# Small attention on one core: the value projection one place later, normalising ahead of it, and the last batch's outputs taken late into two other banks

## The chip, the cores and the metric

The kernel runs on one core of a Trainium2 chip. The metric is the device time of one execution in microseconds (us), as the median of several runs. Below, TensorE is called PE, VectorE DVE, ScalarE ACT, GpSimd POOL, and SyncE, which issues the DMAs, SP.

## The reference, cut to what matters

The reference is a stack of four pairs of cross attention and feed forward over x of 8 x 128 x 512. The change touches one member alone, the small attention of the second pair (L1): 8 batches, 4 patches of 128 columns, 8 heads of width 8.

```python
q = einsum('ed,bdw->bew', Wq, qp) + bq[:, None]      # 64 x 128 of each patch
k = einsum('ed,bdw->bew', Wk, qp) + bk[:, None]
val = einsum('ed,bdw->bew', Wv, vp) + bv[:, None]
scores = einsum('bhdi,bhdj->bhij', qh, kh) / sqrt(dh)
scores = where(mp[:, :, None, :] > 0, scores, -1e9)
o = einsum('bhij,bhdj->bhdi', softmax(scores), vh)
out = einsum('de,bew->bdw', Wo, gelu(o)) + bo[:, None]
x = x + out * masks
```

## The kernel before, in words

The whole program keeps x (8 batches of 128 x 512) in SBUF and runs eight stages one after the other. Each engine has its own instruction stream in program order, written out by hand; semaphores join them. Nothing is reordered by a planner, so a wait that is not met holds everything behind it on its engine.

**The small attention.** Work is cut into 64 units, `UNITS` = 8 for each of 8 batches; unit u is patch n and half s of the heads (4 heads at a time) of batch u // 8. Below, "place i" is u % 8. On PE each place does, in this order: the scores of unit u (L1972); an extra for the next batch (`extras`, L2011); the turning of the probabilities of unit u - 2 (L1980); on even u the values and row sums of the two units u - 4 and u - 3 (L1997, L2000); and at place 6 `spread_inverse` of the batch before (L2008). The extras of the next batch are: places 0 and 1 the keys' projection (L1952), places 2 and 3 the queries' (L1957), place 5 the values' (`project_v`, L1964). `project_v` waits for `q_low`, since it writes the bank proj[0] that DVE's `low_of_queries` reads. The next batch's `project_k` of half 0 writes the same bank and so waits for `v_made`, which DVE's `take_values` gives.

**DVE** does at each place `maxima` (L2181), at odd places `take_turned` (L2187, the copy of the turned probabilities of unit u - 2), then its extras: places 0 and 1 `take_keys` (L2160), place 3 `invert` (L2191), places 4 and 5 `low_of_queries` (L2165), place 6 `take_values` (L2174, L2175) and `norm` (L2153, the input of the batch after next), place 7 `normalise` (L2196). `normalise` of a batch waits for `spread_inverse` and for ACT's `take_outputs`.

**ACT** does `exps` (L2086) at each place, at even places `take_turned` (L2093), and as extras `high_of_keys` (L2073) at 1 and 2, `high_of_queries` (L2078) at 3 and 4, `take_outputs` (L2118) at 5; in batch 3 also three roundings for the next stage at 5, 6 and 7.

**POOL** makes the low parts of the keys (L1915), the live mask (L1897) and the eight blocked key tiles of a batch (L1928), which the scores read. Before the blocks of a batch it waits for the dead-key rows that SP loads (L1861). For the last batch SP issues those rows only after `v_full` has counted all 8 value projections (L1882).

**The end of the stage.** After the last unit PE runs `spread_inverse(7)`, and then `pe_tail` (L596): eight output products (L2049) into outp[0] and outp[1] in turn, each after its product's mask weighing by POOL (L1939), which follows ACT's gelu (L2142), and after DVE's addition two batches before (L500). `out_product(1)` waits for all `onorm`, as outp[1] is also the bank that `normalise(7)` reads. `UNREAD_EXIT` puts four matmuls whose result nobody reads (`unread_passes`, L590: 128x512 of the context into proj[0]) ahead of products 0, 1 and 7. In `dve_tail` (L656) the first half's reciprocal root (`dve_ln_rstd`, scratch in proj[1]) stands between the additions 4 and 5; it waits for ACT's deviations of batches 0 to 3 (L506), which stand behind the gelus in ACT's order.

Of the kernel before, what the change touches and what calls it, by code (L numbers as in the profile page):

```python
# [16 lines left out]
B = 8  # L17
S = 128
D = 512
# [237 lines left out]
def build(nc, ins, out):  # L257

    with ExitStack() as ctx:
# [332 lines left out]
        UNREAD_OUT = {B - 1: 4}  # L592
        UNREAD_EXIT = {0: 4, 1: 4, B - 1: 4}
        UNREAD_TURN = {2: 5, 3: 2}
# [61 lines left out]
        def dve_tail(dve, n, add_of):  # L656
# [7 lines left out]
            if n == 3:  # L664
                dve_ln_rstd(dve, n, 0, proj[1][:, 0:BH], proj[1][:, BH:B])
            else:
                dve_ln_rstd(dve, n, 0)
            for b in range(BH + 1, B):
                add_of(b)
            if n == 3:  # L670
                dve_ln_rstd(dve, n, 1, proj[1][:, B:B + BH], proj[1][:, B + BH:2 * B])
            else:
                dve_ln_rstd(dve, n, 1)
# [1144 lines left out]
        o1 = [flat[0:E1, b * D:(b + 1) * D] for b in range(B)]  # L1818
        turn1, made1 = [turn, outp[0]], [heado, outp[1]]
        tail_mask = [tbuf[0:E1, b, :] for b in range(2)] + [ring[0:E1, 4 + b, :] for b in range(2)] + \  # L1820
# [120 lines left out]
        def l1_pe(pe):  # L1941
# [69 lines left out]
            def extras(b, i):  # L2011
                if b + 1 >= B:
                    return
                if i < 2:
                    project_k(b + 1, i)
                elif i < 4:
                    project_q(b + 1, i - 2)
                elif i == 5:
                    project_v(b + 1)

            for s in range(2):
                project_k(0, s)
# [5 lines left out]
            for u in range(UNITS * B):  # L2028
                scores(u)
                extras(u // UNITS, u % UNITS)  # L2030
                if u >= 2:
                    turn_probabilities(u - 2)
                if u >= 4 and u % 2 == 0:
                    values(u - 4)
                if u >= UNITS and u % UNITS == 6:
                    spread_inverse(u // UNITS - 1)
            u = UNITS * B
# [3 lines left out]
            values(u - 2)  # L2041
            spread_inverse(B - 1)

            def out_product(b):
                if b == 1:
                    pe.wait_ge(m["onorm"], B)
                pe.wait_ge(m["weighed"], b + 1)
                wait(pe, m["added"], b - 1)
                pe.matmul(outp[b % 2][:, :], wo1, flat[0:E1 + 1, b * D:(b + 1) * D], start=True, stop=True)\  # L2049
                  .then_inc(m["out_full"], 1)  # L2050
# [3 lines left out]
        def l1_act(act):  # L2054
# [83 lines left out]
            take_turned(UNITS * B - 2)  # L2138
            take_outputs(B - 1)
            for b in range(B):  # L2140
                act.wait_ge(m["onorm"], b + 1)
                act.activation(o1[b], o1[b], ACT.Gelu, bias=vecs[0:E1, V_BV1:V_BV1 + 1]).then_inc(m["gelu"], 1)  # L2142
# [4 lines left out]
        def l1_dve(dve, add_of):  # L2147
# [50 lines left out]
            def extras(b, i):  # L2198
                if b + 1 < B:
                    if i < 2:  # L2200
                        take_keys(b + 1, i)
                    elif i in (4, 5):
                        low_of_queries(b + 1, i - 4)
                    elif i == 6:
                        take_values(b + 1)
                if b + 2 < B and i == 6:
                    norm(b + 2)
                if b and i == 3:
                    invert(b - 1)
                if b and i == 7:  # L2210
                    normalise(b - 1)

# [20 lines left out]
            invert(B - 1)  # L2233
            normalise(B - 1)

            def add(b):
                dve.wait_ge(m["out_full"], b + 1)
                dve_add_sum(dve, b, outp[b % 2][:, :]).then_inc(m["added"], 1)
                dve.wait_ge(m["added"], b + 1)
# [488 lines left out]
```

## Time and profile before

| what | value |
|---|---|
| runs shown | 2985.66, 2993.47, 2994.1 us; median 2993.47 |
| profiled execution, own time | 2991.93 us |
| span of its trace | 2990.3 us |
| PE busy | 2904.1 us (97%) |
| DVE, ACT, POOL busy | 56%, 38%, 33% |
| mean granted clock of PE | 0.995 of full |
| the small attention in the span | about 1102.4 to 1274.5 us |

The profile is one execution; times in it are counted from the start of its span, and the 1.6 us between its span and its own time lie around the program. The small attention is about 172 us, or 6% of the span. Outside it the program is bound by large products on PE; the change does not touch them.

### The profile page before, as it was taken

The numbers are of one execution on the slowest core, as the hardware profiler recorded it, in microseconds if no ns is written. First come the engines' busy times: TensorE is split into PE (matmuls) and PEld (weight loads), VectorE is DVE, ScalarE is ACT, GpSimd is POOL, SyncE is SP. The second block draws the span as 40 slices with busy tenths as digits, with TensorE's granted clock in tenths as the row PEclk, the third lists the DMA queues.
The fourth block names the chain that finished last, engine by engine and source line by source line (L and its number), as shares of the span: only waits on it lengthen the run. The fifth ranks groups of instructions, "written<-read, shape, count | busy, mean of one in ns | idle before, by whom it ended". The sixth has DMA issues, their size and how long they took to land.

```text
span 2990.3 us, 48856 instructions
## 1 busy us (share of the span) xinstructions
PE 2904.1 (97%) x16710; PEld 2450.0 (82%) x16710; DVE 1682.1 (56%) x3414; ACT 1126.0 (38%) x3642; POOL 988.8 (33%) x822
## 2 busy tenths in 40 slices
PE   7999999999999998899999999999999999999999
PEld 6888888888888866578778888888778888888787
DVE  6544545445452247678766666666764444445644
ACT  4322222222242237732354444444443333333432
POOL 3433333433313227543333222332232333332221
PEclk9999999999999999999999999999999999999999
DMA  3111111111111111011111001110011111110111
GB/s 122 45 49 42 44 34 41 48 41 45 40 36 57 34 45 30 26 39 39 40 40 33 29 28 35 35 35 18 26 57 36 36 35 35 35 35 21 46 49 46
DMA packets 68761, 120.32 MB, mean 40 GB/s; under 512 B 8697, under 2 KB 14329, under 8 KB 68257
## 3 DMA queue, kind: packets, MB, share of 16 engines
q1 hardware_dynamic: 68642, 118.76, 13.0%
q8 instruction: 71, 1.16, 0.2%
q14 instruction: 48, 0.39, 0.0%
HBM read 116.57 MB, written 2.10 MB: 40 GB/s over the span
## 4 chain that ended last, share of the span: by engine, by line
PE 90%; DVE 5%; ACT 2%; issue 2%; POOL 1%; DMA 0%; DVEq 0%; SPq 0%; POOLq 0%; ACTq 0%
PE proj L394 42%; PE outp L394 25%; PE heado L1012 6%; PE score L971 6%; PE turn L998 3%; PE score L394 2%; PE proj L410 1%; PE proj L938 1%; PE score L1558 0%; PE score L1972 0%; PE turn L921 0%; PE proj L1957 0%; PE proj L1952 0%; PE outp L1980 0%; PE outp L1997 0%
## 5 line engine op out<-in xcount | busy, mean ns | idle before, releaser
L394 PE MATMUL outp<-w_out,acts 128*128 128x512 f32 x3288 | 841.3, 400 | 11.0 <-DVE acts L1702 4.4
L394 PE MATMUL proj<-xnT,w_in 128*128 128x512 f32 x3192 | 760.0, 393 | 2.0 <-ACT big L1076 2.0
L394 PEld LDWEIGHTS outp<-w_out,acts 128*128 128x128 f32 x3288 | 594.1, 188 | 140.3 <-DVE x L1697 8.9
L394 PEld LDWEIGHTS proj<-xnT,w_in 128*128 128x128 f32 x3192 | 594.5, 189 | 126.3 <-issue 2.2
L394 PE MATMUL proj<-ctxT,w_kv 128*128 128x512 f32 x1536 | 366.0, 394 | 19.3 <-POOL w_kv L728 18.2
L726 POOL TENSOR_TENSOR w_out<-ring,consts 128x512 fp32r<-128x512 f32 x96 | 102.4, 1067 | 820.8 <-PE outp L394 820.8
L394 PEld LDWEIGHTS proj<-ctxT,w_kv 128*128 128x128 f32 x1536 | 286.7, 189 | 78.4 <-issue 18.1
L1303 DVE TENSOR_TENSOR x<-x,outp 128x512 f32<-128x512 f32 x360 | 244.8, 685 | 181.7 <-PE outp L394 178.6
L1079 DVE COPY big<-proj 128x512 f32<-128x512 f32 x136 | 93.7, 689 | 343.0 <-PE proj L394 338.8
L1076 ACT ACTIVATE big<-proj 128x512 f32<-128x512 f32 x136 | 81.4, 598 | 475.8 <-PE proj L394 469.3
L726 POOL TENSOR_TENSOR w_kv<-ring,consts 128x512 fp32r<-128x512 f32 x93 | 96.6, 1039 | 465.1 <-DMA ring<-in_L_wk 444.6
L1174 ACT ACTIVATE acts<-heado 128x512 fp32r<-128x512 f32 x192 | 114.7, 597 | 309.3 <-PE heado L1012 309.2
L1309 DVE TENSOR_TENSOR acts<-heado,acts 128x512 fp32r<-128x512 f32 x192 | 132.7, 691 | 148.5 <-ACT acts L1174 148.4
L1012 PEld LDWEIGHTS heado<-ptbuf,big 128*128 128x128 f32 x1536 | 200.7, 191 | 17.9 <-ACT ptbuf L1162 1.0
L1162 ACT ACTIVATE ptbuf<-turn 128x512 f32<-128x512 f32 x192 | 114.3, 595 | 266.9 <-PE turn L998 266.8
L1012 PE MATMUL heado<-ptbuf,big 128*128 128x128 f32 x1536 | 202.3, 274 | 1.0 <-DVE acts L1309 1.0
L971 PEld LDWEIGHTS score<-big 128*128 128x128 f32 x1536 | 184.4, 193 | 9.4 <-issue 4.7
L971 PE MATMUL score<-big 128*128 128x128 f32 x1536 | 188.8, 276 | 3.0 <-issue 1.7
L394 PE MATMUL proj<-w_kv,ctxT 128*128 128x256 f32 x1536 | 183.1, 280 | 0.9 <-DVE big L1079 0.9
L394 PEld LDWEIGHTS proj<-w_kv,ctxT 128*128 128x128 f32 x1536 | 182.1, 188 | 2.3 <-DVE big L1079 1.1
L1697 DVE TENSOR_TENSOR x<-x,outp 128x512 f32<-128x512 f32 x152 | 104.2, 686 | 92.1 <-PE outp L394 92.0
L726 POOL TENSOR_TENSOR w_in<-ring,consts 128x512 fp32r<-128x512 f32 x96 | 106.1, 1106 | 118.5 <-PE proj L394 65.8
(338 smaller groups left out, 4093.3 us busy)
## 6 DMA issues: line engine op xcount, KB each, us to landing
ring<-in_L_wq SPq DMA_DIRECT2D x96, 256.0 KB, 2.6
ring<-in_L_wo SPq DMA_DIRECT2D x96, 256.0 KB, 2.6
ring<-in_F_in SPq DMA_DIRECT2D x52, 256.0 KB, 2.7
ring<-in_L_wk SPq DMA_DIRECT2D x48, 256.0 KB, 2.6
ring<-in_L_wv SPq DMA_DIRECT2D x48, 256.0 KB, 3.3
ring<-in_F_out SPq DMA_DIRECT2D x41, 256.0 KB, 2.6
x<-in_x SPq DMA_DIRECT2D x2, 1024.0 KB, 8.0
big<-in_ctxT SPq DMA_DIRECT2D x4, 512.0 KB, 7.6
```

Of the source, the lines that this page charges most:

```text
L394: mm = pe.matmul(bank_ap, w_ap(a, c), rhs(b, c), start=first and c == 0 and n == 0, stop=last and c == chunks - 1 and n == len(PASSES) - 1)
L726: pool.tensor_tensor(dst[:, slot, 0, :], ring[:, r, :], zeros512, ALU.add).then_inc(m["high_w"], 1)
L971: mm = pe.matmul(score[half][:, b * P:(b + 1) * P], qT[:, t], kT[:, t], start=True, stop=True)
L998: mm = pe.transpose(turn[:, b * P:(b + 1) * P], probs[j % 2][:, half, b * P:(b + 1) * P], ident)
L1012: mm = pe.matmul(heado[:, b * P:(b + 1) * P], v_pair[:, n, j % 2, :] if A.own_kv else v[:, n * S:(n + 1) * S], ptbuf[:, half, b * P:(b + 1 ...
L1076: return engine.activation(dst, src, ACT.Copy)
L1079: return engine.tensor_copy(dst, src)
L1162: act.activation(ptbuf[:, half, :], turn[:, :], ACT.Copy).then_inc(m["tfree"], 1)
L1174: act.activation(acts[:, j, 0, half * HALF:(half + 1) * HALF], heado[:, :], ACT.Copy)\
L1303: dve.tensor_tensor(x[:, b, :], x[:, b, :], outp[b % 2][:, :], ALU.add).then_inc(m["added"], 1)
L1309: dve.tensor_tensor(acts[:, j, 1, cols], heado[:, :], acts[:, j, 0, cols].bitcast(F32), ALU.subtract)\
L1697: dve.tensor_tensor(x[:, b, :], x[:, b, :], outp[b % 2][:, :], ALU.add).then_inc(m["added"], 1)
```

## The change

On PE `project_v` moves from place 5 to place 6 and `spread_inverse` from place 6 (behind the values) to place 5 (ahead of the turning). On DVE `take_values` moves from place 6 to place 7, behind `take_turned`, and `normalise` from place 7 to place 6, ahead of `norm`. Eight unread matmuls stand ahead of the first key projection, and those ahead of output products 0 and 1 go. The last batch's `spread_inverse` and `normalise` stand between output products (additions) 1 and 2, its `take_outputs` ahead of its own gelu and behind the seven others. The output products use outp[0] and proj[1] in place of outp[0] and outp[1]; the scratch of the reciprocal root changes places with them.

```diff
--- before.py
+++ after.py
@@ -590,7 +590,7 @@
                 pe.matmul(proj[0][:, :], ctxT[:, 0, 0, 0:P], ctxT[:, 0, 0, 0:HALF], start=True, stop=True)
 
         UNREAD_OUT = {B - 1: 4}
-        UNREAD_EXIT = {0: 4, 1: 4, B - 1: 4}
+        UNREAD_EXIT = {B - 1: 4}
         UNREAD_TURN = {2: 5, 3: 2}
 
         def pe_tail(pe, n, out_of):
@@ -662,13 +662,13 @@
                     add_of(b)
                 return
             if n == 3:
-                dve_ln_rstd(dve, n, 0, proj[1][:, 0:BH], proj[1][:, BH:B])
+                dve_ln_rstd(dve, n, 0, outp[1][:, 0:BH], outp[1][:, BH:B])
             else:
                 dve_ln_rstd(dve, n, 0)
             for b in range(BH + 1, B):
                 add_of(b)
             if n == 3:
-                dve_ln_rstd(dve, n, 1, proj[1][:, B:B + BH], proj[1][:, B + BH:2 * B])
+                dve_ln_rstd(dve, n, 1, outp[1][:, B:B + BH], outp[1][:, B + BH:2 * B])
             else:
                 dve_ln_rstd(dve, n, 1)
             dve_ln_norm(dve, n, 4)
@@ -1816,7 +1816,7 @@
         mask1, dead1 = ring[E1:E1 + B, 4, :], ring[E1:E1 + B, 5, :]
         krows = spare[STACK:ROWS, :].rearrange("p (k s n) -> p k s n", k=2, s=2)
         o1 = [flat[0:E1, b * D:(b + 1) * D] for b in range(B)]
-        turn1, made1 = [turn, outp[0]], [heado, outp[1]]
+        turn1, made1, out1 = [turn, outp[0]], [heado, outp[1]], [outp[0], proj[1]]
         tail_mask = [tbuf[0:E1, b, :] for b in range(2)] + [ring[0:E1, 4 + b, :] for b in range(2)] + \
                     [tail1[0:E1, b * D:(b + 1) * D] for b in range(2)] + \
                     [factors1[0:E1, 14 * P + b * D:14 * P + (b + 1) * D] for b in range(2)]
@@ -2015,9 +2015,10 @@
                     project_k(b + 1, i)
                 elif i < 4:
                     project_q(b + 1, i - 2)
-                elif i == 5:
+                elif i == 6:
                     project_v(b + 1)
 
+            unread_passes(pe, 8)
             for s in range(2):
                 project_k(0, s)
             for s in range(2):
@@ -2028,25 +2029,24 @@
             for u in range(UNITS * B):
                 scores(u)
                 extras(u // UNITS, u % UNITS)
+                if u >= UNITS and u % UNITS == 5:
+                    spread_inverse(u // UNITS - 1)
                 if u >= 2:
                     turn_probabilities(u - 2)
                 if u >= 4 and u % 2 == 0:
                     values(u - 4)
-                if u >= UNITS and u % UNITS == 6:
-                    spread_inverse(u // UNITS - 1)
             u = UNITS * B
             turn_probabilities(u - 2)
             values(u - 4)
             turn_probabilities(u - 1)
             values(u - 2)
-            spread_inverse(B - 1)
 
             def out_product(b):
-                if b == 1:
-                    pe.wait_ge(m["onorm"], B)
+                if b == 2:
+                    spread_inverse(B - 1)
                 pe.wait_ge(m["weighed"], b + 1)
                 wait(pe, m["added"], b - 1)
-                pe.matmul(outp[b % 2][:, :], wo1, flat[0:E1 + 1, b * D:(b + 1) * D], start=True, stop=True)\
+                pe.matmul(out1[b % 2][:, :], wo1, flat[0:E1 + 1, b * D:(b + 1) * D], start=True, stop=True)\
                   .then_inc(m["out_full"], 1)
 
             pe_tail(pe, 3, out_product)
@@ -2136,8 +2136,9 @@
                     take_turned(u - 2)
                 extras(u // UNITS, u % UNITS)
             take_turned(UNITS * B - 2)
-            take_outputs(B - 1)
             for b in range(B):
+                if b == B - 1:
+                    take_outputs(b)
                 act.wait_ge(m["onorm"], b + 1)
                 act.activation(o1[b], o1[b], ACT.Gelu, bias=vecs[0:E1, V_BV1:V_BV1 + 1]).then_inc(m["gelu"], 1)
             ffn_act_first(act, F1)
@@ -2201,14 +2202,14 @@
                         take_keys(b + 1, i)
                     elif i in (4, 5):
                         low_of_queries(b + 1, i - 4)
-                    elif i == 6:
+                    elif i == 7:
                         take_values(b + 1)
+                if b and i == 6:
+                    normalise(b - 1)
                 if b + 2 < B and i == 6:
                     norm(b + 2)
                 if b and i == 3:
                     invert(b - 1)
-                if b and i == 7:
-                    normalise(b - 1)
 
             for b in range(BH + 2):
                 add_of(b)
@@ -2231,11 +2232,12 @@
                     dve_ln_rstd(dve, 2, 1, outp[1][:, 0:BH], outp[1][:, BH:B])
             take_turned(UNITS * B - 1)
             invert(B - 1)
-            normalise(B - 1)
 
             def add(b):
+                if b == 2:
+                    normalise(B - 1)
                 dve.wait_ge(m["out_full"], b + 1)
-                dve_add_sum(dve, b, outp[b % 2][:, :]).then_inc(m["added"], 1)
+                dve_add_sum(dve, b, out1[b % 2][:, :]).then_inc(m["added"], 1)
                 dve.wait_ge(m["added"], b + 1)
 
             dve_tail(dve, 3, add)
```

## Rows read from the trace of the kernel before

**Rows 1.** The page: busy time of each engine, and the chain that ended last.
```profile
PE 2904.1 (97%) x16710; PEld 2450.0 (82%) x16710; DVE 1682.1 (56%) x3414; ACT 1126.0 (38%) x3642; POOL 988.8 (33%) x822
PE 90%; DVE 5%; ACT 2%; issue 2%; POOL 1%; DMA 0%; DVEq 0%; SPq 0%; POOLq 0%; ACTq 0%
```

**Rows 2.** By stretch: length; busy PE, weight loads, DVE, ACT, POOL; clock; DMA, GB/s.
```profile
1130.72:1218.67 87.95, 80.13 (x962) 55.87 (x961) 67.69 (x104) 71.42 (x209) 63.18 (x56) 1.00 0.09 26
...
1268.45:1275.27 6.82, 6.82 (x14) 3.73 (x14) 4.27 (x19) 3.74 (x8) 6.42 (x6) 0.50 0.07 13
```

**Rows 3.** Order of time on PE, one batch: start, length, operation, idle time before it.
```profile
1148.00 1.02 PE L1952 MATMUL proj<-sq,wk 128*96 128x512 f32 x2
...
1158.34 0.49 PE L1972 MATMUL score<-stacks 98*128 98x512 f32 x1
...
1159.83 1.08 PE L1964 MATMUL proj<-biasbuf,ring 128*128 128x64 f32 x8 [0.99 <-DVE stacks L2165]
...
1165.26 1.02 PE L1952 MATMUL proj<-sq,wk 128*96 128x512 f32 x2
```

**Rows 4.** Order of time on DVE, the end of the same batch.
```profile
1156.49 0.69 DVE L2187 COPY ptbuf<-outp 128x512 f32<-128x512 f32 x1 [0.61 <-PE outp L1980]
1157.22 0.96 DVE L2191 RECIPROCAL inverse<-outp 64x128 f32<-64x128 f32 x1
1158.21 0.69 DVE L2181 TENSOR_REDUCE negmax<-score 128x4 f32<-128x512 f32 x1
...
1162.11 0.75 DVE L2165 SCALAR_TENSOR_TENSOR stacks<-proj,biasbuf,stacks 32x512 fp32r<-32x512 f32 x1
1162.89 0.69 DVE L2181 TENSOR_REDUCE negmax<-score 128x4 f32<-128x512 f32 x1
1163.50 0.35 DVE L2174 COPY spread<-proj 128x192 f32<-128x192 f32 x1
...
1164.01 0.64 DVE L2153 TENSOR_SCALAR sq<-x,rstd,recentre 128x512 f32<-128x512 f32 x1
...
1166.11 0.69 DVE L2196 TENSOR_TENSOR big<-big,outp 64x512 f32<-64x512 f32 x1
```

**Rows 5.** Order of time on ACT, the same end of batch.
```profile
1158.93 1.14 ACT L2086 ACTIVATE pbuf<-score,negmax 128x128 f32<-128x128 f32 x4 [0.68 <-DVE negmax L2181]
...
1160.42 0.69 ACT L2078 ACTIVATE stacks<-proj,biasbuf 96x512 fp32r<-96x512 f32 x1
...
1162.46 0.59 ACT L2118 ACTIVATE big<-outp 64x512 f32<-64x512 f32 x1
```

**Rows 6.** Order of time on SP, POOL and PE where the last batch begins.
```profile
1231.61 2.51 SPq L1861 DMA_DIRECT2D spare<-ring  x4
...
1236.34 6.03 POOL L1928 TENSOR_TENSOR stacks<-spare,consts 98x512 fp32r<-98x512 f32 x6 [7.98 <-issue]
...
1237.44 0.56 PE L1972 MATMUL score<-stacks 98*128 98x512 f32 x1 [1.57 <-POOL stacks L1928]
```

**Rows 7.** Busy time by stretch, right behind that wait (columns as in rows 2).
```profile
1237.70:1241.10 3.40, 3.40 (x38) 2.47 (x38) 0.69 (x1) 1.42 (x5) 3.40 (x4) 0.51 0.72 236
```

**Rows 8.** Order of time on PE, the start of the stage and the middle of batch 0.
```profile
1104.44 3.53 PE L1952 MATMUL proj<-sq,wk 128*96 128x512 f32 x4 [2.06 <-DMA pattern<-in_L_pattern]
...
1124.56 1.44 PE L1964 MATMUL proj<-biasbuf,ring 128*128 128x64 f32 x8 [2.84 <-DVE stacks L2165]
```

**Rows 9.** Order of time on ACT, PE and DVE, the end of the stage.
```profile
1254.93 0.60 ACT L2093 ACTIVATE ptbuf<-turn 128x512 f32<-128x512 f32 x1 [0.75 <-PE outp L2000]
...
1258.07 1.28 ACT L2142 ACT_TABLE_LOAD   x1
...
1259.49 1.21 PE L590 MATMUL proj<-ctxT 128*128 128x512 f32 x4
...
1272.55 1.91 PE L2049 MATMUL outp<-big,biasbuf 65*128 65x512 f32 x2
...
1274.56 0.69 DVE L500 SCALAR_TENSOR_TENSOR x<-outp,x 128x512 f32<-128x512 f32 x1 [2.06 <-PE outp L2049]
```

## The prediction

> **What bounds the kernel now.** I read the page first, then the stretches of the stage, then the order of time of one batch on each engine. The page says that PE is busy for 97% of the span and carries 90% of the chain that ended last [rows 1]. So the change can only gain where PE waits inside the small attention, and only lose by making PE wait or run slower there. The five stretches from the key projection of one batch to that of the next, for batches 2 to 7, take 87.95 us at full granted clock with PE busy for 80.13 of them [rows 2]. One undisturbed batch is 1148.00 to 1165.26, or 17.26 us. Its largest hole on PE is ahead of the value projection: the scores of place 5 start at 1158.34 and, by the spacing of such scores, let PE go on 0.34 us later, but the value projection starts at 1159.83, released by DVE's `low_of_queries` [rows 3]. That is 1.15 us, and the trace calls 0.99 of it idle. The reader is to see two more things in these rows. The copy of the values on DVE starts at 1163.50 and takes about 0.56 us (0.51 to the start of `norm`) [rows 4], while the key projection that needs it starts at 1165.26, so it has 1.2 us in hand. And DVE's and ACT's operations of places 3 to 6 follow each other almost without a gap [rows 4, 5].
>
> **The change, part by part.** Times with a + are counted from a batch's first key projection.
>
> *The hole ahead of the value projection.* With `spread_inverse` at place 5, PE has about 1.0 us of work where it waited (its eight matmuls keep the same cost; they only move). The inverse is ready: DVE's reciprocal ran 1157.22 to 1158.18, ahead of the scores of place 5. The turning follows, then the scores of place 6, which wait some 0.2 us for the exponentials of place 4 (ACT 1158.93 plus 1.14, rows 5), and then the value projection finds `low_of_queries` done. PE would reach the next key projection at 17.26 - 1.15 + 0.25 = +16.4. If nothing else were late, five batches would gain 0.9 each, 4.5 us.
>
> *What is late next.* The key projection needs `v_made`. I follow DVE from the last point that PE alone sets, the turning at place 3. It releases `take_turned` at 1156.49 - 1148.00 = +8.49, `invert` starts 0.73 later, `maxima` of place 4 follows after 0.99, ACT's exponentials after 0.72, the queries' high part after 1.49 (with a copy between) and it takes 0.69 [rows 4, 5]. So `low_of_queries` of half 1 starts at +13.15. In the trace it started at 1162.11, +14.11, behind a late `take_turned`, so this is 0.96 earlier. Then come `maxima` of place 6 (at +13.93, 0.61 to the next) and, new here, `normalise`. It needs ACT's `take_outputs`, which follows place 5's exponentials (from about +13.1, 1.02 to the next) and ends at +14.7. So: `normalise` +14.74 (0.72), `norm` +15.46 (0.64), `maxima` of place 7 +16.10 (0.61), `take_turned` +16.71 (0.73), and only then `take_values` +17.44, done at +18.0. I allow 0.1 for the crossing to PE: the key projection starts at +18.1. PE has waited 1.7 us for it, and the batch is 0.87 us longer than before. Behind that wait on PE stand a turning, values and the scores of place 1. From there to place 3 DVE and ACT are earlier relative to PE than before, and PE sets the pace again, so the loop settles at 18.1. Five such stretches give 90.6 against 87.95: **+2.7 us**. Batch 3, where ACT has three more roundings, is already slower and hides a part of its own share. Bounds: -4.5 (the copy never late) and +4.4 (0.87 everywhere).
>
> *The clock.* In the trace one wait of this size stands in the stage: PE idles 1.57 us ahead of the scores of unit 56 [rows 6], and right behind it 3.40 us run at 0.51 of the full clock, the 1.2 GHz level [rows 7]. Work that takes half of that at full clock is done in it, so such a drop costs 1.7 us where PE sets the pace. The waits of 0.99 did not do it: all five stretches show 1.00 [rows 2]. The new wait of 1.7 is nearest to the one of 1.57. But its batch has different work around it each time, and one case is one case: I take three drops of five, **+5.1 us**, bounds 0 and 8.5.
>
> *The start.* PE idles 2.06 us ahead of the first key projection, and the four matmuls behind it take 3.53 us where two of them take 1.02 at full clock [rows 3, 8]. Four matmuls of 128x512 that nobody reads took 1.21 us at the end of the stage [rows 9]; eight fit about into the idle 2.06 and should hold the clock. Two key projections, query projections and their DVE steps then end earlier, and POOL's blocks start about 1.2 us earlier. It does not last. Batch 0 contains a reciprocal root on DVE that holds PE for 2.84 us [rows 8] in either order, and in the new order the values are copied behind `take_turned` there too; by the same steps the next batch's key projection comes out where it was. **0**, bounds -1.3 and +0.6.
>
> *The DMAs of the last batch.* The dead-key rows of batch 7 are queued on SP behind the last value projection: issue at 1231.61, POOL's blocks from 1236.34, the scores of unit 56 at 1237.44 [rows 6]. The value projection ends at +13.66 instead of +12.9, so rows, blocks and scores come 0.7 us later relative to their batch: **+0.7**. PE's wait there grows from 1.57 to about 3.5 us, and the slow stretch behind it may be longer: bounds 0 and +2.4. SP's later loads stand behind these; they are for the next stage, which needs them only behind the gelus.
>
> *The end.* `spread_inverse(6)` no longer stands between values and the scores of unit 63, which brings the last units about 0.95 us forward. ACT can load its gelu table right behind `take_turned` (1254.93 plus 0.60) instead of at 1258.07 [rows 9], so the gelus, and POOL behind them, start 3.5 us earlier. The end of the stage is the addition of batch 7 at 1274.56. It waits for its product, this for addition 5, this for the reciprocal root, this for ACT's deviations of batch 3, and these for the gelu of batch 7, which now waits for `normalise(7)` between additions 1 and 2. With the granted clock at full this walk ends at 1271.5, a gain of 3.1. But without the unread matmuls PE has only short products with gaps between them; the trace had 6.82 us at half clock there even with them [rows 2], where one product took about 1.7 us (1.91 for its two records, rows 9), which is slower than POOL weighs the batches. If the clock is low from the second product on, PE sets the pace with eight products, the spreading and the last four unread ones, and the gain is 0.5. I take a value nearer to that: **-1.2**, bounds -3.1 and +1.7 (one more slow stretch). The two other banks cost nothing and free the first product from `normalise(7)`; the scratch only changes places.
>
> Sum: 2.7 + 5.1 + 0 + 0.7 - 1.2 = **+7.3 us** on the profiled execution's own 2991.93, or 2999.2. The median of the runs shown is 2993.47, 1.5 us above that execution, and the runs spread over 8 us; about 0.3% (9 us) is what a measurement of this kernel can tell from no change. I forecast **2999 us**, no change that can be told, on the slow side of it.
>
> **The rivals.**
> *A. No drops of the clock.* The new wait stays short of what lowers it. For it: the waits of 0.99 never did. Against it: 1.57 did. Sum 2.7 + 0.7 - 1.2 = +2.2, or 2994.
>
> *B. A drop in every batch: slower.* The place is the first key projection of batches 3 to 7; the price is 1.7 us each, 8.5 in all, and it decides once more than three fall. For it: the wait is longer than the one that did it. Sum 2.7 + 8.5 + 0.7 - 1.2 = +10.7, or 3002.6, slower by 0.36%.
> The Trainium skill, "TensorE: Matmul & The Clock Gate", section "A second HAM failure mode: psum-queue depth-cycling", says that PE can swing between its two clock levels when it idles briefly and often between groups of matmuls. By that rule every batch would pay, as in B. The trace so far goes against it at 0.99 us of idle per batch.
>
> *C. The copy is not late: faster.* DVE's chain has slack that I do not see, PE keeps the 4.5 us, the start keeps 1.3 and the end 3.1: -8.9, or 2983.0, faster by 0.30%. Against it: the steps above add up rows that follow each other without gaps, and 1.7 us would have to be wrong.
>
> *D. The reordering does nothing*, as its waits are all covered elsewhere: 2992. PE's share of the chain speaks against it.
>
> **How the numbers follow.** Forecast with some drops 0.36, A 0.26, B 0.22, C 0.12, D 0.04. C comes out at the bound, so with the runs' own spread, and a little for what no case names, about 0.11 is faster by over 0.3%. B, and the forecast where it falls high, give 0.30 slower; 0.59 is within. The range takes in A, B and most of C, with the bounds of the end: 2984 to 3007.
>
> **What would show it.** Right: the value projection without a DVE wait ahead of it; ahead of L1952 in each batch a wait of 1.5 to 1.9 us released by DVE's `take_values` (L2175 before); batches of 18.1 us; half clock behind some of these waits; at the start full clock; the wait for POOL ahead of unit 56 near 3.5 us; the gelu table load ahead of the last `take_outputs`. Wrong: batches below 17 us, which would mean that DVE reaches the copy earlier than the walk says; full clock throughout, which leaves A; or a stage that ends over 3 us earlier, counted from its last values, which would mean that the end is worth more than I gave it.

## The result, and the profile after

The changed kernel takes 3028.5 us (median of 4 runs, 3021.49 to 3032.6) against 2993.48 for the kernel before: 1.0121 of its time, 95% interval 1.0094 to 1.0147. It is slower by some 35 us, and the forecast of 2999 with its range up to 3007 missed it. The profiled execution of the changed kernel took 3032.6 us, its span 3031.0.

The page of the changed kernel, which answers to [rows 1], with the total above them and the first PE group of its costliest groups (busy time, mean ns, idle time ahead of it and what ended it):

```profile
span 3031.0 us, 48854 instructions
PE 2924.6 (96%) x16710; PEld 2463.7 (81%) x16710; DVE 1679.3 (55%) x3414; ACT 1125.3 (37%) x3642; POOL 988.9 (33%) x822
q14 instruction: 73, 0.60, 0.1%
PE 87%; DVE 6%; issue 3%; ACT 2%; POOL 1%; DMA 0%; DVEq 0%; SPq 0%; ACTq 0%; POOLq 0%
L394 PE MATMUL outp<-w_out,acts 128*128 128x512 f32 x3288 | 848.9, 402 | 32.3 <-DVE x L1303 24.2
```

The same lines of the kernel before, for the total, the queue that carries instructions (packets, MB, share) and that group:

```profile
span 2990.3 us, 48856 instructions
q14 instruction: 48, 0.39, 0.0%
L394 PE MATMUL outp<-w_out,acts 128*128 128x512 f32 x3288 | 841.3, 400 | 11.0 <-DVE acts L1702 4.4
```

The numbers of matmuls and of DVE, ACT and POOL operations are the same as in [rows 1]. What differs is odd for a change of order in the small attention: PE now idles 32.3 us ahead of output products of the *large* members (L394), 24.2 of it for DVE's addition L1303; "issue", time in which an engine waits for nothing that the profile shows, goes from 2% to 3% of the chain; and the queue that brings instructions moved 73 packets, where it moved 48.

The waits (engine, what it did next, whom it waited for: us in all, times, longest) say where. First the stretch 1640 to 2182 us of the changed kernel, which is the attention with 8 groups of 4 heads behind F1:

```profile
ACT pbuf L1136 <- DVE negmax L1254: 38.2, 12, 7.1
DVE pbuf L1248 <- issue: 31.8, 5, 6.8
PEld outp L394 <- DVE x L1303: 25.5, 13, 5.0
PE outp L394 <- DVE x L1303: 22.6, 7, 4.8
```

and the same of the kernel before (1600 to 2140):

```profile
ACT pbuf L1136 <- DVE negmax L1254: 9.1, 13, 0.9
DVE pbuf L1248 <- DVE rq L442: 3.9, 12, 0.6
PE outp L394 <- DVE x L1303: 1.0, 2, 0.9
```

DVE stands still 5 times, 31.8 us together, ahead of L1248, and ACT and then PE wait behind it. The order of time on DVE shows one of them, and the starts of all five:

```profile
1687.06 0.17 DVE L442 SCALAR_TENSOR_TENSOR rq<-heado,rq 128x8 f32<-128x8 f32 x1
1693.28 1.13 DVE L1248 SCALAR_TENSOR_TENSOR pbuf<-score,rq,maskadd 128x128 f32<-128x128 f32 x4 [6.05 <-issue]
1694.44 0.69 DVE L1254 TENSOR_REDUCE negmax<-pbuf 128x4 f32<-128x512 f32 x1
...
1781.18 1.13 DVE L1248 SCALAR_TENSOR_TENSOR pbuf<-score,rq,maskadd 128x128 f32<-128x128 f32 x4 [6.83 <-issue]
...
1867.75 1.13 DVE L1248 SCALAR_TENSOR_TENSOR pbuf<-score,rq,maskadd 128x128 f32<-128x128 f32 x4 [6.72 <-issue]
...
1954.72 1.12 DVE L1248 SCALAR_TENSOR_TENSOR pbuf<-score,rq,maskadd 128x128 f32<-128x128 f32 x4 [6.11 <-issue]
...
2040.89 1.13 DVE L1248 SCALAR_TENSOR_TENSOR pbuf<-score,rq,maskadd 128x128 f32<-128x128 f32 x4 [6.13 <-issue]
```

They are 86 to 88 us apart, one for each round of the loop that runs groups 1 to 6 of this attention. Six rounds have five jumps back, and this L1248 is the first operation of the loop's body. PE shows it as some 5 us more of idle time in each 100 (columns as in [rows 2]). The kernel before has

```profile
1700.00:1800.00 100.00, 99.04 (x571) 85.71 (x571) 63.06 (x178) 46.38 (x214) 31.72 (x27) 1.00 0.11 31
```

and the changed one

```profile
1700.00:1800.00 100.00, 94.33 (x531) 81.77 (x530) 60.61 (x175) 41.19 (x187) 23.70 (x20) 0.96 0.10 27
1800.00:1900.00 100.00, 94.47 (x520) 81.35 (x519) 57.48 (x160) 42.20 (x188) 23.68 (x20) 0.97 0.08 27
```

The granted clock (third number from the end) is lower as well. Over the five stretches from 1600 to 2100, PE idles 26.8 us in the changed kernel and 5.2 in the one before, and the clock is 0.96 to 0.98 where it was 1.00. So some 22 us of the loss are PE's idle time; the rest is work behind these waits at the lower clock, by my estimate from these rows 14 us (500 us at 0.03 less).

From the first L1248 of this attention to its last, the kernel before takes 601.8 us (1515.9 to 2117.7), the changed one 635.7 (1524.5 to 2160.2). That is 33.9 of the 40.7 us between the two spans, in a stage whose text the change does not touch. A further 8.6 lie ahead of it, 2.8 of them ahead of the first key projection's start in the small attention (1104.44 against 1107.24), and e6, which has no part of the change there, starts as late (1107.36).

**The theory.** The page's total is 2 instructions lower (48854 for 48856). Counted in the compiled program, one of them is PE's, a dropped wait, and the other is DVE's. In the changed kernel the two waits of `normalise(B - 1)` share one wait instruction, and the addition behind it has lost one of its two waits to the normalising ahead of it and needs no instruction for the other. So everything on DVE behind the small attention lies one instruction earlier, the loop of 264 instructions too (its register addition and its jump are counted). It is the only loop outside PE's program that is longer than 256; DVE's other four have 66 to 142. Theory M: DVE keeps a part of its program at hand and loads the rest in blocks. At this start the loop no longer fits in what is kept, and each jump back must load again. The Trainium skill, "Runtime: NRT & Kernel Launch", section "Instruction fetch mechanics", says that most engines (TensorE has more) hold 512 instructions, in two blocks of 256, and that a taken jump to what is not held waits for a load. By that rule 264 instructions touch three blocks from 7 of 256 starts. The rival, N: what the small attention does differently reaches the later stage as a shift in time.

### The profile page after: what moved, and what is told of

Same layout as the page of the kernel before. It is cut to its first block, busy times and chain, and to the rows that moved or that the text cites. A ratio compares the mean times of both kernels' runs of the same rounds, so it can differ in the third digit from the quotient of the medians.

```text
span 3031.0 us, 48854 instructions
## 1 busy us (share of the span) xinstructions
PE 2924.6 (96%) x16710; PEld 2463.7 (81%) x16710; DVE 1679.3 (55%) x3414; ACT 1125.3 (37%) x3642; POOL 988.9 (33%) x822
## 4 chain that ended last, share of the span: by engine, by line
PE 87%; DVE 6%; issue 3%; ACT 2%; POOL 1%; DMA 0%; DVEq 0%; SPq 0%; ACTq 0%; POOLq 0%
PE proj L394 40%; PE outp L394 24%; PE heado L1012 6%; PE score L971 5%; PE turn L998 3%; PE score L394 2%; PE proj L410 1%; DVE pbuf L1248 0%; PE score L1558 0%; PE score L1972 0%; ACT acts L1174 0%; PE proj L1952 0%; DVE acts L1309 0%; PE heado L1997 0%; PE proj L1957 0%
## 5 line engine op out<-in xcount | busy, mean ns | idle before, releaser
L394 PE MATMUL outp<-w_out,acts 128*128 128x512 f32 x3288 | 848.9, 402 | 32.3 <-DVE x L1303 24.2
L394 PE MATMUL proj<-xnT,w_in 128*128 128x512 f32 x3192 | 761.2, 394 | 2.0 <-ACT big L1076 2.0
L394 PEld LDWEIGHTS outp<-w_out,acts 128*128 128x128 f32 x3288 | 598.6, 190 | 164.4 <-DVE x L1303 28.4
L394 PEld LDWEIGHTS proj<-xnT,w_in 128*128 128x128 f32 x3192 | 595.5, 189 | 126.6 <-issue 2.3
L394 PE MATMUL proj<-ctxT,w_kv 128*128 128x512 f32 x1536 | 366.8, 395 | 19.6 <-POOL w_kv L728 18.6
L394 PEld LDWEIGHTS proj<-ctxT,w_kv 128*128 128x128 f32 x1536 | 287.1, 189 | 79.1 <-issue 18.6
L1303 DVE TENSOR_TENSOR x<-x,outp 128x512 f32<-128x512 f32 x360 | 244.2, 685 | 183.8 <-PE outp L394 180.7
L394 PE MATMUL proj<-w_kv,ctxT 128*128 128x256 f32 x1536 | 183.1, 280 | 0.9 <-DVE big L1079 0.9
L394 PEld LDWEIGHTS proj<-w_kv,ctxT 128*128 128x128 f32 x1536 | 182.0, 188 | 2.3 <-DVE big L1079 1.1
```

The source lines that it names most:

```text
L394: mm = pe.matmul(bank_ap, w_ap(a, c), rhs(b, c), start=first and c == 0 and n == 0, stop=last and c == chunks - 1 and n == len(PASSES) - 1)
L1303: dve.tensor_tensor(x[:, b, :], x[:, b, :], outp[b % 2][:, :], ALU.add).then_inc(m["added"], 1)
```

## The experiments

The last column is the time from the first L1248 of that attention to the last, from the two ends in each profile. "DVE ahead" is the number of DVE's instructions ahead of its loop, counted in the compiled programs, against the kernel before. In the session of e13 to e15 the kernel before took 2992.82 us, one run.

| run | DVE ahead | loop | time to before (95%) | issue ahead of L1248, us, times | q14 packets | L1248 first to last |
|---|---|---|---|---|---|---|
| before | 0 | 264 | 1 | none | 48 | 601.8 |
| after | -1 | 264 | 1.0121 (1.0094, 1.0147) | 31.8, 5 | 73 | 635.7 |
| e1 after, one wait more | 0 | 264 | 1.0034 (1.0023, 1.0044) | none | 48 | 600.5 |
| e2 before, one wait less | -1 | 264 | 1.0103 (1.0086, 1.0120) | 30.7, 5 | 73 | 631.8 |
| e3 before | -11 | 264 | 0.9997 (0.9987, 1.0006) | none | 47 | 600.6 |
| e4 after, one more behind the loop | -1 | 264 | 1.0124 (1.0106, 1.0141) | 31.2, 5 | 73 | 632.9 |
| e9 before, unread start | -9 | 264 | 1.0002 (0.9993, 1.0012) | none | 47 | 600.5 |
| e10 before | -8 | 264 | one run, 2990.42 | none | 47 | 600.5 |
| e13 before | -7 | 264 | one run, 3011.97 | 27.4, 10 | 72 | 627.3 |
| e14 before | +248 | 264 | one run, 3012.3 | none | 49 | 600.4 |
| e15 before | +249 | 264 | one run, 3044.34 | 27.5, 10 | 74 | 630.6 |
| e11 after, shorter loop | -1 | 248 | 1.0018 (1.0009, 1.0027) | none | 47 | 601.5 |
| e16 before, shorter loop | 0 | 248 | 1.0000 (0.9991, 1.0009) | none | 47 | 599.9 |

### One instruction

e1 is the changed kernel with one wait that is long met:

```diff
             take_turned(UNITS * B - 1)
+            dve.wait_ge(m["sfull"], UNITS * B)
             invert(B - 1)
```

> The changed kernel with one more DVE instruction, a wait that is long met, ahead of the last reciprocal of the small attention. Theory M (instruction fetch): the change leaves DVE's program one wait instruction shorter, which moves the 264-instruction loop of the big attention that follows across a boundary of the instruction store, and each of the 5 jumps back then waits some 6.4 us (31.8 us in 5 in the changed kernel's waits). M expects that wait gone and about 2997 us (3028.5 less 32). Rival N (what the small attention does differently reaches the later stage as a shift in time): one wait that is met at once changes nothing, 3028 us with the 5 waits still there.

e2 is the kernel before with one wait less, in `norm`:

```diff
-                dve.wait_ge(ln_rms, centred(2, b // BH))
+                if b != 2:
+                    dve.wait_ge(ln_rms, centred(2, b // BH))
```

> The kernel before with one DVE wait instruction fewer (the input of batch 2 no longer waits for the reciprocal root that batch 0 has already waited for); nothing else of the change. M expects 5 waits of 6.4 us ahead of L1248 and about 2993.5 + 32 = 3025 us. N expects no such wait and 2993 us.

e3 drops this wait for five batches, and in the last additions six waits of DVE on its own additions (`if b in (BH, B - 1)` ahead of the trailing wait on `added`).

> The kernel before with 11 DVE wait instructions fewer (waits that an earlier wait of DVE has met already). M with a store refilled in blocks of 256: a loop of 264 touches three blocks only for the 8 or 9 starts just ahead of a boundary, so minus one to minus nine would be slow and minus eleven is back at about 2993 us with no wait. If instead every shorter program were slow, it would be some 3025 us. N expects 2993 us, as for minus one.

e4 has two waits on L1's `added` and `out_full` ahead of the last additions of the attention behind the loop, which make one more instruction there.

> Control: the changed kernel with one more DVE wait instruction behind the loop of the big attention in place of ahead of it, so the program is as long as in the kernel before but the loop lies where it does in the changed one. M expects 3028 us with the 5 waits; only if the program's whole length counted would it be 2997 us. N expects 3028 us too.

e1 takes 2997.55 us, 31 less than the changed kernel, for one instruction more; e4, timed beside it, takes 3026.29, so 28.7 more than e1. The group of L1248 in its profile (idle time ahead of it, times):

```profile
  DVE rq L442: 6.5, 25
```

e2, which has nothing of the change, pays for one instruction less:

```profile
  issue: 30.7, 5
  DVE rq L442: 3.7, 20
```

M holds in all four and N in neither of the two where they differ. PE's program is one instruction shorter in e1 too, which is clean, and not in e2, which is slow, so its length is not the cause. e3 says that a shorter program is not slow by itself, and e4 that the whole length does not count, only what stands ahead of the loop.

### Which starts are slow

e10 and e13 leave out eight and seven of e3's waits (five of `norm`, and three and two of the additions); e14 and e15 add them:

```diff
             take_turned(UNITS * B - 1)
+            for k in range(248):
+                dve.wait_ge(m["sfull"], UNITS * B)
+                dve.wait_ge(m["exps"], UNITS * B)
             invert(B - 1)
```

> The kernel before with 8 met DVE wait instructions fewer. It marks the edge of the bad starts beside minus nine and minus eleven: if the jump at the loop's end counts (265 instructions), three blocks are still touched and the 5 waits are there (about 3020 us); if 264 count, it is clean (about 2990 us). If both minus eight and minus nine are clean, M holds but the edge lies nearer to minus one.

> The kernel before with 7 met DVE wait instructions fewer. Minus one is slow and minus eight is clean. If the store is refilled in blocks of 256 and the loop's 264 instructions are what must fit into two blocks, starts minus one to minus seven are slow and minus eight is the first clean one: 5 waits of 6 to 7 us ahead of L1248, about 3020 us. If the slow starts are only the one or two next to the boundary (a first instruction too late in its block), minus seven is clean at 2990 us.

> The kernel before with 248 more DVE wait instructions, all met, ahead of the last reciprocal of the small attention: that costs DVE some time there, the same within a wait as in plus 249. Blocks of 256: 248 more is minus eight of the next block, so no wait of 6.4 us ahead of L1248. Blocks of another size (128, 512): nothing special at either of the two.

> As plus 248 with one more. Blocks of 256: 249 more is minus seven of the next block, so 5 waits of 6 to 7 us ahead of L1248 and some 31 us more than plus 248. Blocks of 512: as plus 248, no such wait. Blocks of 128 would have shown at plus 121 and be silent here unless the loop needed two of a different count: then both or neither.

Minus seven is slow and minus eight is clean (e3's and e9's expectations had put the edge one or two further); plus 249 is slow and plus 248 is clean. The additional waits of e14 cost time at their own place (the last normalising starts at 1284.0 in place of 1259.6), in e15 as well; between the two lie 32.0 us for one instruction. So slow starts were seen at -1, -7 and +249, clean ones at 0, -8, -9, -11 and +248, and the pattern comes again after 256. That is what two blocks of 256 and a body of 264 give if the loop of the kernel before starts on the first instruction of a block (its place in the store is inferred from the pattern, not read): up to seven earlier leave 257 or more for the blocks behind, and eight earlier fit again. The Trainium skill's rule, in the section named above, agrees with these starts to the instruction.

At -7 and +249 the wait is split. e13's group of L1248 has

```profile
  issue: 27.4, 10
```

and in the order of time the first of its rounds:

```profile
1676.76 1.13 DVE L1248 SCALAR_TENSOR_TENSOR pbuf<-score,rq,maskadd 128x128 f32<-128x128 f32 x4 [4.36 <-issue]
1679.72 1.13 DVE L1248 SCALAR_TENSOR_TENSOR pbuf<-score,rq,maskadd 128x128 f32<-128x128 f32 x4 [1.11 <-issue]
```

Seven instructions at the end of a block give DVE something to do before it needs the next block; with one it waits some 6.4 us in one piece. That the split comes from two loads one after the other is my reading of it.

### The loop's length

e11 is the changed kernel, its loop at the same bad start, but 16 instructions shorter:

```diff
-                m.wait(dve, "added", B * p + (b - B + 1))
+                if A.layer != 2 or isinstance(p, int):
+                    m.wait(dve, "added", B * p + (b - B + 1))
```

> The changed kernel, its loop of the big attention at the same start, but the loop 248 instructions long in place of 264: inside it DVE's additions no longer wait for its own additions of 8 steps before (PE's products already wait for them). M: two blocks hold 248 instructions at that start, so the 5 waits go, and it is 2997 us or a little less (16 instructions in each of 6 rounds fewer). If the start by itself is what costs (its first instruction the last of a block), the waits stay and it is 3028 us.

> The kernel before with the shorter loop of e11 (248 instructions in place of 264, DVE's additions in the big attention not waiting for its own of 8 steps before). At before's start the loop was clean already, so the theory of the store expects no gain from that; what is left is 16 instructions fewer in each of 6 rounds on an engine that PE seldom waits for: 0 to -0.001 of before. If the shorter loop is what took the changed kernel from 1.0034 (with the wait) to 1.0018 (with the short loop), this one is 0.998 to 0.999; if that difference was scatter, it is 1.000.

The waits are gone at the bad start: the length of the body, with its start, decides. With blocks of 256, a body of up to 257 would fit two blocks from every start, an estimate from the edges above, so this repair does not hang on what stands ahead. e16 shows that the 16 instructions are worth nothing by themselves (1.0000).

### The parts of the change

These were made at clean starts, so they show what the change does in its own stage.

> The kernel before with only the value projection a place later (and the spread of the inverse, the values' copy and the normalising moved as in the change); the start, the end and the banks are those of before, and DVE's program keeps its length. My prediction's steps: +2.7 us for the wait of the next key projection on the values' copy, +5.1 for clock drops, so about 2990 + 6 to 8. The marks of the changed kernel (last key projection 120.9 after the first, where before has 117.4) say +3.5 to +4. If the move is a gain by itself (the start or the end of the stage being the loss), it would be 2987 or less.

> The kernel before with only the end changed: last batch's outputs taken late, output products in the two other banks, no unread matmuls ahead of products 0 and 1; one met DVE wait keeps the program's length. My prediction's step: -1.2 us (bounds -3.1 and +1.7). The marks of the changed kernel say -2.4 up to the first output product and +4 to +4.4 from there to the last one, so +1.5 to +2.

> As the end alone, but the 4 unread matmuls ahead of output products 0 and 1 stay. If the loss at the end is the half clock of the products (1.06 us each where before has 0.68), this one keeps the clock up and has the gain of the late outputs alone: 1 to 2.5 us faster than before. If the loss is the new order (normalising the last batch behind the first additions), the unread matmuls change nothing and it is as the end alone, +1.5 to +2.

> The changed kernel with one met DVE wait (program length of before) and DVE's copy of the values ahead of its copy of the turned probabilities at place 7. My prediction's rival C: the key projection then does not wait (some 1.0 us less in each of the 7 batches, up to 5 us in all, and fewer clock drops), so 4 to 8 us below the changed kernel with the wait alone (1.0034 of before), i.e. 0.9993 to 1.001 of before. If what costs is the turned copy, which PE's values wait for, it moves the hole there and the time stays at 1.003.

> The kernel before with the 8 unread matmuls ahead of the first key projection as its only part of the change, and 9 met DVE wait instructions fewer. My prediction's step for the start: 0 (bounds -1.3 and +0.6). What the parts leave open: the changed kernel with the wait is 1.0034 of before, the value move alone 1.0019, the end alone 0.9998, so the start would be +0.0015 or +4.5 us if parts add. Theory M with a store in blocks of 256 and a loop of 264 or 265: nine fewer is the first start at which two blocks hold the loop again, so no wait of 6.4 us ahead of L1248.

> Value projection at place 6 with DVE's copy of the values ahead of its turned copy, the late outputs in the two other banks with the unread matmuls ahead of products 0 and 1 kept, no unread matmuls at the start, and the shorter loop of e11. By the parts: copy ahead 0 to -1, end -1 to 0, start 0, the loop's 16 fewer instructions 0 to -3, so 0.998 to 1.000 of before. If the parts don't add (the phase of the stages behind shifts), 1.000 to 1.002.

> The kernel before with the value move of e5 and DVE's copy of the values ahead of its turned copy, and nothing else. e5 is 1.0019 with stretches of 17.78 us; in e8 they were 17.18 with the copy ahead (before: 17.26). So 7 batches at -0.1 us: 0.999 to 1.000 of before. If the wait of the key projection was not what made e5 slower, it stays at 1.002.

e5, e6 and e9 are the hunks of the change one at a time; e7 is e6 with `UNREAD_EXIT` as before. The copy ahead, in e8, e12 and e17, is this, with `take_values` gone from place 7 of `extras`:

```diff
                 maxima(u)
+                if u % UNITS == 7 and u // UNITS + 1 < B:
+                    take_values(u // UNITS + 1)
                 if u >= 2 and u % 2:
                     take_turned(u - 2)
```

| run | time to before (95%) | five stretches, us | last scores to first L1558 of the next stage |
|---|---|---|---|
| before | 1 | 87.95 | 35.5 |
| e1 whole change, clean start | 1.0034 (1.0023, 1.0044) | 91.65 | 37.5 |
| e5 value move alone | 1.0019 (1.0010, 1.0027) | 90.01 | 34.3 |
| e6 end alone | 0.9998 (0.9989, 1.0006) | 87.92 | 37.5 |
| e7 end, unread kept | 1.0001 (0.9992, 1.0010) | 87.97 | 34.6 |
| e8 whole change, copy ahead | 1.0004 (0.9996, 1.0013) | 87.58 | 37.6 |
| e9 start alone | 1.0002 (0.9993, 1.0012) | 87.92 | 34.2 |
| e12 copy ahead, end with unread, short loop | 1.0001 (0.9992, 1.0010) | 87.60 | 34.7 |
| e17 value move, copy ahead | 1.0014 (1.0005, 1.0023) | 89.23 | 37.3 |

The value move is the part that costs, 5.7 us (0.0019 of 2989). That is a little less than the 6 to 8 of my steps and more than the 3.5 to 4 that the key projections in the changed kernel's trace had said. The end and the start cannot be told from zero (-3.3 to +1.8 us, and -2.1 to +3.6); for the end I had expected +1.5 to +2. With the new order of the end, the unread matmuls of the exit hold the clock, as the stretch of the output products shows (the clock is the third number from the end), in e6, which leaves those ahead of products 0 and 1 out:

```profile
1260.50:1278.00 17.50, 17.47 (x30) 8.05 (x31) 7.65 (x28) 11.03 (x24) 13.31 (x11) 0.51 0.09 30
```

and in e7, which has them:

```profile
1257.70:1272.00 14.30, 11.27 (x37) 5.49 (x38) 8.02 (x29) 10.05 (x23) 13.26 (x11) 1.00 0.07 18
```

By the profiles they are worth 2.9 us at the end of the stage (37.5 against 34.6), but the timed runs do not tell e7 from e6, so my expectation of 1 to 2.5 us below before was wrong there. The column's 35.5 for the kernel before is one execution: in nine profiles whose end is that of the kernel before it lies between 34.2 (e9, e13) and 37.3 (e17), by which of its products run at half clock (so with the order of before the same matmuls do not hold it each time). So a comparison with one profile of before says little, while the 37.5 to 37.6 (e1, e6, e8) and the 34.6 to 34.7 (e7, e12) repeat. With the copy ahead, e8's stretches come out at 87.58, just below before's, and the time is before's. e17 has the same copy and is 1.0014; its profile has one stretch where the first key projection and the next are 4.41 us apart (1201.64 to 1206.05) where the others need 2.79, that is one clock drop of 1.6 us. My expectation was 0.999 to 1.000. Its interval and e8's overlap, and why it should lie above e8 by more than that drop is open. So is why the whole change at a clean start is 1.0034 with the long loop and 1.0018 with the short one (these intervals overlap too), when the parts sum to 1.0019 and e16 gives the short loop nothing. No version beats the kernel before by what can be measured.

## Why the prediction was wrong, point by point

**The step that failed** is the sentence ahead of the sum: "the change can only gain where PE waits inside the small attention, and only lose by making PE wait or run slower there". The sum had no term for an engine's instruction stream outside the stage. One DVE instruction less put the 264-instruction loop of a later attention on a bad start, where five jumps back wait 31.8 us, for 26 to 31 us of the time (1.0121 against e1's 1.0034 is 26 us; the medians of the two, 3028.5 and 2997.55, differ by 31; e4 less e1 is 28.7, and e2's 1.0103 is 30.8). The walk should have counted what the change adds and drops in each engine's program, waits too, and looked behind the stage for loops near the limit. None of the rivals had it either: B, the slower one, is a clock rule.

**Inside the stage** the sum of +7.3 us stands against +10.2 (e1, interval 6.9 to 13.2) and +5.4 (e11, 2.7 to 8.1). Its steps, in the changed kernel's trace:

*Late copy of the values.* The order came out as walked. DVE at the end of a batch whose first key projection is at 1134.49, against [rows 4]:

```profile
1149.26 0.69 DVE L2197 TENSOR_TENSOR big<-big,heado 64x512 f32<-64x512 f32 x1
1149.87 0.54 DVE L2154 TENSOR_SCALAR sq<-x,rstd,recentre 128x512 f32<-128x512 f32 x1
1150.43 0.69 DVE L2182 TENSOR_REDUCE negmax<-score 128x4 f32<-128x512 f32 x1
1151.04 0.68 DVE L2188 COPY ptbuf<-outp 128x512 f32<-128x512 f32 x1
1151.64 0.35 DVE L2175 COPY spread<-proj 128x192 f32<-128x192 f32 x1
```

`normalise` is at +14.77 (walked +14.74) and `take_turned` at +16.55 (+16.71); the copy is at +17.15 where I had +17.44, because `norm`, `maxima` and the copy follow the operations ahead of them at 0.61, 0.56 and 0.60 us where I took 0.72, 0.64 and 0.73. PE, against [rows 3]:

```profile
1168.31 0.47 PE L1972 MATMUL score<-stacks 98*128 98x512 f32 x1
1170.04 1.07 PE L1952 MATMUL proj<-sq,wk 128*96 128x512 f32 x2 [1.25 <-DVE spread L2176]
```

The stretch is 17.78 us (1152.26 to 1170.04), not 18.1, and the wait 1.25, not 1.7. The value projection no longer waits (in all batches L1964 waited 9.8 us for L2165 in the kernel before, and 1.1 in the changed one, in one batch), so the hole was closed and a larger one opened behind it, as predicted.

*The copy never late (rival C)* is what e8 makes: with DVE's two copies changed about, 17.18 us per stretch. C gave the stage 4.5 us for it; it got 0.4 (87.95 less 87.58), since PE still waits 0.66 us for the copy.

*The clock.* This is the mis-sized term inside the stage: three drops of five, +5.1, was too many, and the length of the wait was the wrong guide. In the trace of after, five stretches (against the first of [rows 2]):

```profile
1134.49:1224.95 90.46, 82.53 (x961) 56.76 (x961) 67.08 (x106) 71.06 (x208) 62.15 (x55) 0.98 0.10 25
```

All four waits of 1.25 us here have full clock behind them; the one drop stands in batch 3, where PE waited 0.35. In e1 one wait of 1.25 has half clock behind it (its stretch takes 19.39 in place of 17.78, so 1.6 us, about the 1.7 that I had taken from [rows 7]), and in e5 none. In all, the stretches cost +2.1 with no drop (e5), +2.5 and +3.7 with one (after, e1), and +4.1 and +5.1 with two (e4, e11), where the prediction had +7.8. So the waits came to +2.1 for my +2.7, and the drops to 0 to +3.0 for my +5.1: between rival A and the forecast.

*The start.* Not to be told from zero, as timed (1.0002). The eight unread matmuls (1105.11, 1.99 us) fill the idle time of [rows 8] and the four key projections take 1.96 us in place of 3.53. This does not show that the unread matmuls hold the clock: the projections take 1.93 us in e3, e6, e12 and e17 too, which have no such matmuls ahead of them, and 2.96 to 3.56 in before, e2, e5 and e7. In the middle of batch 0 PE still waits 2.82 us (2.84 before), now ahead of the scores, whose exponentials stand behind the reciprocal root:

```profile
1105.11 1.99 PE L590 MATMUL proj<-ctxT 128*128 128x512 f32 x8
1107.24 1.96 PE L1952 MATMUL proj<-sq,wk 128*96 128x512 f32 x4
...
1126.67 0.65 PE L1972 MATMUL score<-stacks 98*128 98x512 f32 x1 [2.82 <-ACT pbuf L2086]
```

*The dead-key rows.* PE waits 3.55 us (predicted 3.5) where [rows 6] has 1.57:

```profile
1244.41 0.80 PE L1972 MATMUL score<-stacks 98*128 98x512 f32 x1 [3.55 <-POOL stacks L1928]
```

From the last key projection to the last scores it is 30.0 us before and 30.2 to 30.5 with the change: +0.2 to +0.5 for my +0.7.

*The end.* The table load for the gelus stands ahead of the last `take_outputs`, as said, and the first output product comes 2.4 us earlier after the last scores. Then they all run at half clock:

```profile
1266.96 2.08 PE L2049 MATMUL proj<-big,biasbuf 65*128 65x512 f32 x2
1268.97 1.97 PE L2008 MATMUL outp<-inverse,pattern 64*64 64x128 f32 x8
1270.86 2.08 PE L2049 MATMUL outp<-big,biasbuf 65*128 65x512 f32 x2
```

That is the case I had described and priced at -0.5; the products take 16.4 us from first to last where before has 11.8. In the traces the end is 37.5 to 37.6 against 35.5, so +2.0, above my bound of +1.7; but the kernel before's own end moves between 34.2 and 37.3, and timed alone the change of the end cannot be told from zero. The reordered end has the mechanism that I gave it, but not the gain.

## What to carry to other kernels

Count the instructions of each engine's loops, waits, register arithmetic and the jump among them. A body that does not fit two blocks of the instruction store from every start (here, DVE's of 264) is a bet on its place, and a change elsewhere in the program, by one wait, can lose it. Before reading a surprising difference as work, compare the packets of the instruction queue and look for "issue" ahead of the first operation of a loop; then put the lost instruction back, or make the body shorter. And an A/B comparison of two orders means little until both have the loop at a clean start: here the stage itself cost 0.2 to 0.3%, the place of a loop elsewhere 1.0%.

## What the runs showed of the hardware

A jump back at a bad start, read here as one to a part of the program that DVE no longer holds, costs 5.7 to 6.8 us of idle time at a start of minus one (after, e2, e4), and 4.2 to 4.6 plus 1.0 to 1.5 at minus seven and plus 249 (e13, e15). It shows in no operation's duration (the medians of L1248 are 342 and 343 ns in the changed kernel and 342 and 343 in the one before). Each such jump moved on average 5 packets and some 42 KB on the instruction queue (73 less 48 packets and 0.60 less 0.39 MB, by five). The slow starts recur after 256 instructions, and the idle time falls from 27.4 us to nothing between a start of minus seven and one of minus eight. Here nothing hid it, since scores, exponentials and PE's output products all wait for DVE at the loop's head. PE's loops are longer (422 and 496 instructions in the two later attentions, 657 in the first, counted in the compiled program), and in the waits of that attention PE's and its weight loads' longest "issue" is 0.8 us in the kernel before and in the changed one; the Trainium skill, in the section named above, gives TensorE room for 2048 instructions, which no run here tests.

TensorE's clock did not follow the length of the wait ahead of it. In the five traces with the late copy (after, e1, e4, e5, e11), it fell from the 2.4 GHz level to that of 1.2 behind 3 of 17 waits of 1.25 to 1.26 us (granted 0.52 to 0.55 over the next 3.4 us), behind 1 of 3 waits of 2.05 to 2.08, and behind 2 of 5 waits of only 0.35, in the batch with three more roundings on ACT.
